# A graph layer on one core: masks and counts of the nodes made in the edge stage, totals by a backward maximum, the last adds on another engine

## What is computed

```python
h = maximum(layernorm(x), 0)                    # x: 50000 x 256
msg = relu(h[src] + edge_attr)                  # 25000 edges x 256
p = msg @ W_fc.T + b_fc                         # 25000 x 256
scores = p @ Q.T                                # 4 heads
w = exp(scores - segment_max(scores, dst)[dst])
alpha = w / maximum(segment_sum(w, dst)[dst], 1e-9)
pooled[:, h] = segment_sum(alpha[:, h:h+1] * p, dst)
mean_p = segment_sum(p, dst) / maximum(deg, 1)  # deg: edges of a node
gate = softmax(mean_p @ Wg.T + bg)              # 4 per node
out = x + sigmoid(sum over h of gate[:, h] * pooled[:, h])
```

## Time and profile before

| what | value |
|---|---|
| median of 3 runs | 744.5 us (744.27 to 744.82) |
| profiled execution | 740.5 us, span 738.8 us |
| mean granted TensorE clock | 0.934 |
| PE busy | 553.3 us (75%) |
| DVE busy | 487.2 us (66%) |
| ACT busy | 383.7 us (52%) |
| POOL busy | 440.3 us (60%) |
| moved | 171.53 MB, mean 232 GB/s |

### The profile page before, as it was taken

One profiled execution on the slowest core, in us unless ns is written; L12 is line 12 of the kernel. 1 busy time (PEld: TensorE's weight loads), 2 busy tenths in 40 slices (PEclk: granted clock), 3 DMA queues, 4 the chain that ended last, 5 costly groups with the idle time before them and its releaser, 6 DMA issues.

```text
span 738.8 us, 12420 instructions
## 1 busy us (share of the span) xinstructions
PE 553.3 (75%) x2474; PEld 435.4 (59%) x2475; DVE 487.2 (66%) x1651; ACT 383.7 (52%) x661; POOL 440.3 (60%) x334
## 2 busy tenths in 40 slices
PE   3418988988889867989003998889888778877775
PEld 2206866766668656767002876777666666655554
DVE  4118677868679767878998766666565655554552
ACT  2105455646557455664130244666766575666663
POOL 7765556666651655640000256677878787778887
PEclk9999899989999999999655999999999999999998
DMA  7434455555553577775000799999999999999998
GB/s 222 136 92 145 142 163 172 169 167 171 169 173 117 162 230 254 242 256 188 25 0 3 251 361 366 307 305 324 358 327 340 335 345 316 320 332 343 336 340 277
DMA packets 137238, 171.53 MB, mean 232 GB/s; under 512 B 10096, under 2 KB 123784, under 8 KB 137202
## 3 DMA queue, kind: packets, MB, share of 16 engines
q10 hardware_dynamic: 91344, 90.23, 37.2%
q1 hardware_dynamic: 33010, 42.70, 18.2%
q0 software_dynamic: 12848, 38.20, 16.2%
HBM read 111.50 MB, written 59.60 MB: 232 GB/s over the span
## 4 chain that ended last, share of the span: by engine, by line
PE 46%; DVE 14%; issue 9%; ACT 8%; another core or an unknown queue 7%; POOL 6%; ACTq 4%; DMA 2%; DVEq 2%; POOLq 0%; SPq 0%
PE bank L726 23%; PE bank L809 16%; POOL arena L444 6%; PE bank L716 5%; ACT arena L583 5%; DVE spread L1196 3%; ACTq L586 2%; ACT bank L559 2%; DVE p_keep L997 1%; ACTq L538 1%; DVE stats L977 1%; DVEq L1200 1%; ACTq L591 1%; DMA p_keep<-in_x_dram,idx 1%
## 5 line engine op out<-in xcount | busy, mean ns | idle before, releaser
L809 PE MATMUL bank<-p_keep,spread 128*128 x1172 | 273.4, 387 | 54.4 <-DVE spread L1196 46.1
L444 POOL TENSOR_TENSOR arena<-arena 128x1024 f32<-128x1024 f32 x96 | 224.7, 2350 | 144.0 <-ACT arena L583 143.6
L809 PEld LDWEIGHTS bank<-p_keep,spread 128*128 128x128 f32 x1172 | 217.4, 191 | 111.2 <-issue 84.2
L1196 DVE TENSOR_SCALAR spread<-bank,rel,wgt 128x128 f32<-128x128 f32 x586 | 195.8, 403 | 130.9 <-PE bank L809 78.7
L726 PE MATMUL bank<-w_all,arena 128*128 128x264 f32 (+1 forms) x784 | 232.1, 423 | 43.2 <-ACT arena L491 22.3
L726 PEld LDWEIGHTS bank<-w_all,arena 128*128 128x128 f32 (+1 forms) x784 | 146.1, 207 | 68.7 <-ACT arena L491 36.3
L583 ACT ACTIVATE arena<-bank 128x1024 f32<-128x1024 f32 x97 | 99.2, 1022 | 144.8 <-PE bank L809 131.9
L431 POOL DMA_INDIRECT p_keep<-in_x_dram,idx x124 | 120.4, 971 | 71.6 <-issue 32.6
L491 ACT ACTIVATE arena<-bank 128x256 f32<-128x256 f32 x196 | 72.9, 373 | 103.9 <-remote 51.4
L431 POOL DMA_INDIRECT arena<-in_x_dram,idx x72 | 70.1, 974 | 60.8 <-ACT arena L483 33.9
L559 ACT ACTIVATE bank<-zero 128x1024 f32<-128x1024 f32 x98 | 100.5, 1026 | 3.0
(11 more groups left out here) (197 smaller groups left out, 163.7 us busy)
## 6 DMA issues: line engine op xcount, KB each, us to landing
out_dram<-arena ACTq DMA_DIRECT2D x97, 512.0 KB, 4.5
arena<-in_x_dram ACTq DMA_DIRECT2D x73, 512.0 KB, 5.4
arena<-in_edge_attr_dram SPq DMA_DIRECT2D x48, 512.0 KB
arena<-in_x_dram POOLq DMA_DIRECT2D x24, 512.0 KB, 5.7
p_spill<-p_keep SPq DMA_DIRECT2D x16, 512.0 KB
p_keep<-p_spill SPq DMA_DIRECT2D x16, 512.0 KB, 5.5
p_keep<-in_x_dram,idx POOLq DMA_INDIRECT x124
arena<-in_x_dram,idx POOLq DMA_INDIRECT x72
```

The costliest lines, as they stand in the source:

```text
L444: pool.tensor_tensor(yout[:, slot, :, :], yout[:, slot, :, :], xin[:, slot, :, :], ALU.add).then_inc(summed, 1)
L809: nc.tensor.matmul(places[:, bass.ds(place, T)], spread[:, k0 + k, :], p_rows[:, bass.ds(p_at, T)], start=False, stop=True, skip_group_che ...
L1196: v.tensor_scalar(spread[:, k, :], bank[:, 7, P:2 * P], rel[:, bass.ds(s0 + k, 1)], wgt[:, bass.ds(s0 + k, 1)], ALU.is_equal, ALU.mult).th ...
```

## The change

- `node_work(k)` is new: the operations that need only `dst` (`joins`, `neg`, end-of-tile masks, negated masks, `in_first`, `in_last`, the subtracted column for the spreads) stand in iterations k = 60 to 100 of DVE's edge loop. In place of the ninth row the count of edges comes there from two scans of `joins` (forward with a sum, backward with a maximum); `less` holds minus one over the count. These tiles lie in `spread` and no longer in `arena`.
- In the serial stage the scans start after 4, 8 and 16 transposes, not 8 and 16. The backward scan of the weights takes the maximum of the running sums, without mask. The four gate rows are masked, and negated, by one three-operand operation.
- DVE's two words of the table are loaded before it waits for the weight sums; PE's first 12 steps stand ahead of its loop, and the first 6 wait for one spread each and not for three.
- The adds of the last two groups are taken by DVE behind its last spread.

```diff
             same, same_next = joins[:, 0:RW], joins[:, 1:RW + 1]
...
+            def node_work(k):
+                b = k % 2
+                blk = slice(b * P, (b + 1) * P)
+                if k == 60:
+                    v.memset(joins[:, 0:RW + 1:P], 0.0).then_inc(node_step, 1)
+                elif k == 62:
+                    v.tensor_tensor(per_blk(same)[:, :, 1:P], dst_f[:, :, 1:P], dst_f[:, :, 0:P - 1], ALU.is_equal
+                                    ).then_inc(node_step, 1)
...
+                elif k in (78, 79):
+                    v.tensor_tensor_scan(in_first[:, blk], same[:, blk], ones[:, :], 0.0, ALU.mult, ALU.add
+                                         ).then_inc(node_step, 1)
+                elif k in (82, 83):
+                    dve.wait_ge(node_step, 12)
+                    v.tensor_tensor_scan(less[:, blk][:, ::-1], same_next[:, blk][:, ::-1], in_first[:, blk][:, ::-1], 0.0,
+                                         ALU.mult, ALU.max).then_inc(node_step, 1)
...
+                elif k in (88, 89):
+                    dve.wait_ge(node_step, 15)
+                    v.reciprocal(less[:, blk], less[:, blk]).then_inc(node_step, 1)
...
-            v.tensor_scalar(bank[:, 7, P:2 * P], column[:, :], dst_0, None, ALU.subtract)
-            v.memset(joins[:, 0:RW + 1:P], 0.0)
-            then(v.tensor_tensor(per_blk(same)[:, :, 1:P], dst_f[:, :, 1:P], dst_f[:, :, 0:P - 1], ALU.is_equal))
-            v.memset(tot[:, 0, :], 1.0)
-            v.tensor_scalar(neg, joins, 1.0, BIG, ALU.subtract, ALU.mult)
...
-            dve.wait_ge(rows_turned, 1)
+            dve.wait_ge(node_step, 23)
             for n in range(H):
+                if n % 2 == 0:
+                    dve.wait_ge(rows_turned, n // 2 + 1)
                 ins = v.tensor_tensor_scan(w_run[:, n, :], neg_same, row(n), 0.0, ALU.add, ALU.max)
             then(ins)
-            dve.wait_ge(rows_turned, 2)
+            dve.wait_ge(rows_turned, 3)
...
-                v.tensor_tensor_scan(run[:, n, :], same, row(n), 0.0, ALU.mult, ALU.add)
-            v.tensor_tensor_scan(run[:, K, :], same, tot[:, 0, :], 0.0, ALU.mult, ALU.add).then_inc(rows_read, 1)
-            v.tensor_scalar(cneg, cm, 1.0, BIG, ALU.subtract, ALU.mult)
-            v.tensor_scalar(wneg, one_node, 1.0, BIG, ALU.subtract, ALU.mult)
-            v.tensor_scalar(end, same_next, -1.0, 1.0, ALU.mult, ALU.add)
+                ins = v.tensor_tensor_scan(run[:, n, :], same, row(n), 0.0, ALU.mult, ALU.add)
+            ins.then_inc(rows_read, 1)
+            dve.wait_ge(rows_read, 1)
+            v.scalar_tensor_tensor(run[:, H:K, :], same_next.unsqueeze(1).broadcast_to([P, H, RW]), 1.0, run[:, H:K, :],
+                                   ALU.subtract, ALU.mult)
...
-            then(v.tensor_tensor(run, run, end.unsqueeze(1).broadcast_to([P, C, RW]), ALU.mult))
...
-            for n in range(C):
+            for n in range(K):
                 ins = v.tensor_tensor_scan(tot[:, n, ::-1], same_next[:, ::-1], run[:, n, ::-1], 0.0,
-                                           ALU.mult, ALU.add)
+                                           ALU.mult, ALU.max if n < H else ALU.add)
...
-            deg = run[:, 8, :]
-            then(v.tensor_scalar(deg, tot[:, K, :], 1.0, None, ALU.max))
-            then(v.reciprocal(deg, deg))
-            then(v.tensor_tensor(run[:, 0:H, :], tot[:, H:K, :], over_h(deg), ALU.mult))
+            then(v.tensor_tensor(run[:, 0:H, :], tot[:, H:K, :], over_h(less), ALU.mult))
...
-            for b in range(BLK):
-                v.tensor_scalar(in_first[:, b * P:(b + 1) * P], dst_f[:, b, :], dst_f[:, b, 0:1], None, ALU.is_equal)
-                v.tensor_scalar(in_last[:, b * P:(b + 1) * P], dst_f[:, b, :], dst_f[:, b, P - 1:P], None, ALU.is_equal)
...
             dve.wait_ge(words_in, 64)
-            for h in range(2):
-                need(h)
-                spreads(0, h * HALF, HALF)
+            first, second = need_word(0), need_word(1)
+            dve.wait_ge(p_ready, first & 255)
+            dve.wait_ge(zeroed, first >> 8)
+            dve.wait_ge(wgt_summed, 1)
+            then(v.tensor_copy(wgt[:, 0:P], bank[:, 7, 2 * P:3 * P]))
...
-            with pe.Fori(0, TURNS) as turn:
+            steps(0, 0, 0, HALF, 1)
+            steps(1, 0, HALF, HALF)
+            with pe.Fori(1, TURNS) as turn:
...
+            slot = (FULL - 1) % 4
+            dve.wait_ge(sig_done, FULL)
+            dve.wait_ge(x_pool[slot], 16 * ((FULL - 1) // 4))
+            v.tensor_tensor(yout[:, slot, :, :], yout[:, slot, :, :], xin[:, slot, :, :], ALU.add).then_inc(last_summed, 1)
```

More of the change, by code:

```diff
@@ L98, in gnn_layer @@
     BY_POOL = (0,)
+    assert FULL % 4 == 1 and (FULL - 1) % 4 in BY_POOL
     assert PERIOD % SLOTS == 0 and PERIOD % XS == 0 and LAST_WHOLE == 2 and N % P and FULL % PERIOD == 1
@@ L796, in _, with steps @@
             p_rows = p_keep[:, :, :].rearrange("p t d -> p (t d)")
-            def steps(half, s0, k0, n):
+            def steps(half, s0, k0, n, apart=3):
                 _, words = nc.values_load_multi_w_load_instructions(
@@ L971, in table_work @@
                     dve.wait_ge(next_in, 80)
-                    v.tensor_copy(next_f[:, :, :], next_i[:, :, :])
+                    v.tensor_copy(next_f[:, :, :], next_i[:, :, :]).then_inc(node_step, 1)
+            same, same_next = joins[:, 0:RW], joins[:, 1:RW + 1]
+            neg_same, neg_next = neg[:, 0:RW], neg[:, 1:RW + 1]
+            per_blk = lambda a: a.rearrange("p (b e) -> p b e", b=BLK)
+            for_b = lambda a: a.unsqueeze(2).broadcast_to([P, BLK, 2])
+            for_k = lambda a, k: a.unsqueeze(3).broadcast_to([P, BLK, 2, k])
```

138 lines of the change are left out of this document (82 added, 56 removed).

## The result

The changed kernel takes 735.55 us (median of 4 runs, 731.54 to 738.12) against 744.38 us (median of 4, 743.83 to 744.82) in the same comparison: ratio 0.9878, 95% interval 0.9843 to 0.9913.

The account below looks back on a forecast made before the run. Edge stage to some 345 us, then a serial DVE stage, then a transfer-limited step stage; 6.5 + 0.2 + 1.7 - 2.5 = 5.9 us shorter, from 744.5 to 738.6 us, range 735.9 to 742.6.

Parts of the forecast that it names:

- edge term: Edge stage, iterations 60 to 100: 22 moved DVE operations, 5.9 us of work, cost 2.5 us, bounds 0 and 5.9.
- Nothing later gives it back: Edge stage after iteration 100: the 2.5 us lost is not won back, as the rest runs at the same two paces.
- all added DVE work hides: Rival, edge stage: all added DVE work fits in the 15.5 us of idle time, giving 736.1 us; chance 0.17.
- Serial stage: DVE-only stage from 355 to 400 us and its front: node operations moved out or removed make it 6.5 us shorter.
- The front: Start of the serial stage: scans start after four of PE's transposes, gaining 0.9 us.
- The counts and masks: Serial stage: 0.91 us of operations go, a three-operand pass of 1.3 us replaces them; loss 0.4, at worst 1.5.
- 43.4: Microseconds forecast from the first scan to PE's weight sums, instead of 49.0.
- Opening: Start of the step stage: earlier table loads and shorter waits for spreads gain 0.2 us, bounds -0.5 and +0.5.
- Tail: Kernel's end: DVE takes the last two groups' adds from POOL, gaining 1.7 us, bounds 1.0 and 1.9.
- even if it had to wait for POOL: Tail: DVE's 128x1024 add would end at 732.2 if it waited for POOL, instead of some 731.6.
- More low-clock episodes: Rival, edge stage: PE's waits for late adds bring further low-clock episodes, 4.7 us each; two give 748.0 us; chance 0.05.
- The transfers did not absorb the gain: Answers a rival: transfers end the step stage when they did, only the tail gains, 745.3 us; chance 0.03.

Follow-up runs that it names:

- second series: Follow-up runs on chip 9, including the moved operations done twice and run early; the kernel before took 665.05 us.
- the fourth: Series of follow-up runs on chip 9, with the doubled operations at an early and a later place; the kernel before took 663.63 us.
- long form: Runs of the first series and third series, in which the kernel before took 743 us; the 744.4 us of the result are of this kind.
- edge_triple: Kernel before with the 22 moved operations each done three times in iterations 60 to 100, nothing taken out: 746.05 us against 742.53, ratio 1.004.
- short form: Runs of the second series and the fourth, both on chip 9, in which the same kernel before took 664 to 665 us.
- after_third: The changed kernel, unchanged, run again on chip 9: 655.63 us, ratio 0.9854 to the kernel before.
- nodes_early: Changed kernel with all moved operations but the subtracted column in iterations 6 and 7 of the edge loop: 655.34 us, ratio 0.9848 to the kernel before.
- nodes_serial: Changed kernel with the 22 moved operations at the start of the serial stage instead of the edge stage: 738.48 us, ratio 0.9947 to the kernel before.
- after_again: The changed kernel, unchanged, run again: 734.14 us against 742.99 for the kernel before, ratio 0.9899.
- edge_late: Kernel before with the 22 moved operations each done twice, in iterations 150 to 190: 748.87 us against 742.53, ratio 1.0076.
- first series: Follow-up runs of the parts of the change by themselves; the kernel before took 742.99 us.
- third series: Follow-up runs with the moved operations tripled, doubled at a later place, or with gathers of 64 rows; the kernel before took 742.53 us.

## Why the prediction was right or wrong

**The forecast was too small by its edge term.** The step that failed is "I take 2.5 us", and its reason "Nothing later gives it back: the rest of the stage runs at the same two paces." Measured, by the ratios: +0.7 us for the operations once, +0.7 for twice in the second series (+1.5 in the fourth), -0.4 for taking them away from there; all of these hold 0 within their intervals. Three times cost +3.0 us, at most 5.8, which leaves at most 1.9 for each. Of the 2.5 us nothing can be shown.

Why it failed: I took the paces of PE and DVE for the limit. The pace at full clock, 1.12 us a tile with DVE busy 16.8 of 17 us, is what DVE can do. The stage as a whole does 1.47 us a tile. I had both numbers, and gave the difference of 0.35 us a tile to PE's episodes alone, with a lead of at most 1 us in each. What the runs show in place of the 2.5 us depends on the form. In the long form, in which the forecast was made, the gaps where the work stands take it in: 14.4 to 16.2 us of them from tile 60 to 100, 10.0 to 12.1 with the operations once, and DVE reaches tile 100 no later beyond what such profiles differ. So the 15.5 us of idle time in the earlier trace rows were of use, and "minus at most 1" an episode was too little. Later catch-up is needed there only for more work: `edge_triple` takes 68.4 us from tile 60 to 100, some 5 us more, and its last add is 0.8 to 1.4 us later than those of this form's usual 345.0 to 345.6. In the short form the work does not hide where it stands: DVE is 6.1 us late at tile 100 in `after_third` and on time at the end, since whoever is late keeps 0.11 us of catch-up on each of the 95 tiles behind iteration 100, some 10 us for 5.9 us of work. That refutes "Nothing later gives it back". The rival "all added DVE work hides" gave 736.1 us, 0.55 above the median; I gave it 0.17, for an argument about local order at full clock.

**The range.** Low ends: the own sum with the best bounds gave 735.6, and I cut it to 735.9. The larger miss is the scatter. I took 4 us between profile and median as equal for both kernels and wrote that the median moves by 1.5 us. Executions of either kernel spread with a standard deviation of 3 us, so a median of four can move by about 2 and the range had to be wider on both sides than the costs made it.

**Serial stage: 6.5 forecast, 6.3 measured.** The front gave 0.7 for 0.9. The counts and masks lost 1.15 - 0.91 = 0.24 for 0.4 (L1118 to the link L1125 against L1078 to L1087). The choice for the three-operand form, 1.3 us by L888, was right: 1.22 us for 1024 elements, and 0.29 between starts of the 128-element form (twelve in 3.49), so the 0.35 of L1180 holds a fixed part. The rule of the Trainium skill (Vector Engine (DVE) Microarchitecture Reference, Points that are easy to get wrong) that it runs at half throughput is not borne out by L1118. The rest follows from the 43.38 us that 43.4 had announced.

**Opening: 0.2 forecast, 0.43 measured, by another way.** I expected the hole before the second dozen to close and the first step to stay at once behind the sums. The first step does stand there (400.77, the sums end at 400.94). But the hole is still open, 0.63 us and 0.53 before. The gain is that PE ends its sums and first 24 steps sooner relative to the start of the sums: the second batch begins 9.63 us after it, not 10.06. Both are within the bounds, in single executions.

**Tail: 1.7 forecast, 1.7 measured.** DVE's add took 1.55 us, not 1.23: it started 0.47 us before POOL's add of group 95 ended (727.73 + 2.36 = 730.09) and ended 1.08 us behind that end. The other five profiles with this tail show the same 1.07 to 1.08 us, with adds of 1.54 to 2.07 us by how early they start. So DVE's add got nothing done while POOL's ran, the case of the forecast's "even if it had to wait for POOL". The stores followed at 4.0 us instead of 4.2. (The three stores sum to 1.39 MB, not 1.36, which is 4.2 us for 4.1 and changes nothing.)

**Later and earlier again.** More low-clock episodes did not decide: PEclk in iterations 60 to 100 falls at 154.6 and 188.7 us in after, twice, where I had called over three wrong. The transfers did not absorb the gain: from the first to the last sigmoid the five profiles with the changed step stage (the changed kernel, `nodes_early`, `nodes_serial`) need 315.0 us on average, the nine with before's step stage and whole gathers 315.5, a difference well inside their scatter.

With the edge term at 0 the sum of measured terms is 6.3 + 0.4 + 1.7 = 8.4 us; the three comparisons measured 8.8, 8.9 and 9.4 by medians (9.1, 7.5 and 9.7 by the ratios), with intervals of 2.6 to 2.7 us to each side. What is left is inside them and stays open.

The 4.34 us by which the last edge add of after was late in the first pair of profiles is not the edge term: from tile 114 to 165 after was within about a microsecond of before, in both directions, and the 4 us arose at tiles 170 to 172, a hundred microseconds behind the last moved operation; 342.8 is the earliest last add of this form, and `after_again` has the last add at 345.8.

## What to carry to other kernels

Work put on a busy engine costs what that engine cannot win back before the stage ends. First look for gaps at the place itself. Then compare its time per tile when it never waits with the stage's time per tile, and multiply by the tiles that are left. That product is what it can win back at most: it came out in the short form, and in the long form `edge_triple` and `edge_late` paid 3.0 and 5.6 us though it (95 and 45 tiles at 0.35 us, 33 and 16 us) exceeded their work. So put such work early; in the last quarter of the stage the same work cost half of its length (5.6 of 10.9 us) to two thirds (7.1 of 10.5). Before a term is read from two single profiles, ask how far two profiles of one kernel differ at that place.

## What the runs showed of the hardware

- The same program has an edge stage of 266 or of 345 us, by the series (266 in both on chip 9), with a step stage from first to last sigmoid that is alike (313.95 and 315.1 us before). In the long form the engines pause for 2 to 5.4 us, often with no releaser on the core, in all kernels; in the pause looked at the DMA engines stood at 0 for its last 1.4 us. PE's pause that ends at 102.8 to 105.5 us comes at the same place of its program (behind its 254th recorded matmul) in all six kernels profiled up to the first series, whatever was added to DVE; in the third series two of the four kernels have it. In the short form PE and DVE have none of over 1.2 us from 60 to 130 us.
- A gather's issue on GpSimd took 0.98 us on average for 128 rows and 0.99 us for 64, with 0.30 us to the next. Fewer gathers, not smaller ones, remain to be tried; no run here has them.
- From first to last sigmoid the fourteen profiles with whole gathers give 310.0 to 318.3 us. Much of the scatter of 3 us between executions can come from there.
- An addition of 128x1024 on DVE, both inputs in SBUF, that starts while GpSimd adds in SBUF ends 1.07 to 1.08 us behind the end of GpSimd's add, in all six profiles with such a pair, however early it starts (1.54 to 2.07 us long; 1.22 to 1.23 alone).
- The three-operand form of 128x1024 on DVE, f32 from SBUF, took 1.22 us, as long as the plain multiply.
